# Audio tower on one Trainium2 core: features split 128 + 64 instead of 96 + 96, five matmuls for a product instead of six, router in tiles of 128 tokens

## What is computed

```python
def reference(x, tok_W, tok_b, Wq, Wk, Wv, W_qkv, b_qkv, W_gate, b_gate, A, B_lora, W_proj, b_proj):
    h = einsum('bnf,ef->bne', patches(x), tok_W) + tok_b            # 128 clips, 46 tokens, 192 features
    y = layernorm(h)
    h = h + softmax(causal((y @ Wq) @ (y @ Wk).T)) @ (y @ Wv)
    y = layernorm(h)
    w, idx = top_k(softmax(y @ W_gate.T + b_gate), 2)               # router over 8 experts
    down = einsum('td,nrd->tnr', y, A)                              # 8 experts, rank 16
    qkv = y @ W_qkv.T + b_qkv + 2 * sum_over_chosen(w * (down @ B_lora.T))
    q, k, v = heads(qkv, 12)                                        # 16 features a head
    return h + concat(softmax(q @ k.T / 4) @ v) @ W_proj.T + b_proj
```

## Time and profile before

| | |
|---|---|
| time, median of 3 runs | 698.73 us (697.73 to 700.97) |
| profiled execution | 698.22 us |
| its span, first to last instruction | 696.4 us |
| TensorE busy (share of the span) | 633.9 us (91%) |
| VectorE, ScalarE, GpSimd busy | 521.9, 360.4, 380.7 us |
| mean granted TensorE clock | 0.957 of full speed |

### The profile page before, as it was taken

The page is one execution under the profiler, slowest core; times in us unless marked ns, Lnnn a source line. Parts: engine busy times, 40 slices in busy tenths (PEclk is TensorE's granted clock), DMA queues, the critical chain, the costliest instruction groups (busy, mean ns, idle before and its releaser), DMA issues.

```text
span 696.4 us, 21319 instructions
## 1 busy us (share of the span) xinstructions
PE 633.9 (91%) x8262; PEld 573.4 (82%) x8262; DVE 521.9 (75%) x1365; ACT 360.4 (52%) x670; POOL 380.7 (55%) x634
## 2 busy tenths in 40 slices
PE   2687798999999999999999999999999999977774
PEld 1477788898989898989999898989898988775663
DVE  4352465889788888888888888888878888896662
ACT  2554455666565646565656556565656444533220
POOL 5658876767575666656666666676757322121010
PEclk9999899999999999999999999999999999997755
DMA  9846748675767585848484857666673515251500
GB/s 208 163 92 138 170 92 154 161 125 140 127 156 122 141 140 134 149 114 163 103 176 82 191 88 185 90 173 110 151 123 98 73 43 84 70 80 39 76 26 17
DMA packets 74709, 82.95 MB, mean 119 GB/s; under 512 B 9932, under 2 KB 60016, under 8 KB 74608
## 3 DMA queue, kind: packets, MB, share of 16 engines
q1 hardware_dynamic: 74608, 81.58, 57.7%
HBM read 50.19 MB, written 13.57 MB: 92 GB/s over the span
## 4 chain that ended last, share of the span: by engine, by line
PE 81%; DVE 7%; SPq 4%; POOL 3%; issue 2%; ACT 1%; DMA 1%; DVEq 0%; POOLq 0%; ACTq 0%
PE ps_r L1182 14%; PE ps_r L1184 13%; PE ps_r L1183 13%; PE ps_tok L1182 7%; PE ps_p L1401 6%; PE ps_tok L1183 6%; PE ps_tok L1184 6%; PE ps_s L1389 5%; SPq L393 3%; PE ps_r L1307 3%; PE ps_r L1429 2%; PE ps_r L1318 1%; PE ps_r L1239 1%; DVE p2T L911 1%; DMA xs<-xe 1%
## 5 line engine op out<-in xcount | busy, mean ns | idle before, releaser
L576 POOL TENSOR_TENSOR xs<-raw,xs 90x368 f16<-90x368 f32 x192 | 166.3, 886 | 77.3 <-ACT xs L661 77.3
L1182 PE MATMUL ps_tok<-w_tok,xs 128*128 128x192 f16 x576 | 145.8, 253 | 7.4 <-DMA xs<-xe 4.1
L1184 PE MATMUL ps_tok<-w_tok,xs 128*128 128x192 f16 x576 | 144.5, 251 | 0.0
L1183 PE MATMUL ps_tok<-w_tok,xs 128*128 128x192 f16 x576 | 144.5, 251 | 0.0
L661 ACT ACTIVATE p2T<-ps_p 128x768 f16<-128x768 f32 x64 | 51.9, 810 | 70.0 <-PE ps_r L1184 38.2
L661 ACT ACTIVATE xs<-raw 90x736 f16<-90x736 f32 x96 | 75.3, 805 | 0.0
L1182 PEld LDWEIGHTS ps_tok<-w_tok,xs 128*128 128x128 f16 x576 | 66.4, 115 | 9.8 <-issue 6.8
L1183 PEld LDWEIGHTS ps_tok<-w_tok,xs 128*128 128x128 f16 x576 | 67.1, 117 | 0.2
L1184 PEld LDWEIGHTS ps_tok<-w_tok,xs 128*128 128x128 f16 x576 | 66.4, 115 | 0.2
L911 DVE SCALAR_TENSOR_TENSOR p2T<-ps_p,p2T 128x768 f16<-128x768 f32 x64 | 61.3, 958 | 5.8 <-ACT p2T L661 4.7
L576 POOL TENSOR_TENSOR xe<-raw,xe 90x368 f16<-90x368 f32 x64 | 55.5, 887 | 15.5 <-ACT xe L661 15.3
(11 more groups left out here) (188 smaller groups left out, 2129.1 us busy)
## 6 DMA issues: line engine op xcount, KB each, us to landing
raw<-x SPq DMA_DIRECT2D x32, 1035.0 KB, 7.7
qk_scratch<-qk SPq DMA_DIRECT2D x32, 276.0 KB, 3.1
q<-qk_scratch SPq DMA_DIRECT2D x48, 138.0 KB, 8.4
k<-qk_scratch SPq DMA_DIRECT2D x48, 138.0 KB, 9.0
xs<-xe SPq DMA_DIRECT2D x32, 184.0 KB
v<-v2s SPq DMA_DIRECT2D x64, 73.3 KB
out<-h2b SPq DMA_DIRECT2D x16, 276.0 KB
xs<-xe SPq DMA_DIRECT2D x16, 149.5 KB
```

What stands on the lines that cost most here:

```text
L576: nc.gpsimd.tensor_tensor(lo, src, hi, ALU.subtract).then_inc(s_lo, 1)
L1182: mm(dst, stat[0], mov[0], start=start, stop=False)
L1183: mm(dst, stat[0], mov[1], start=False, stop=False)
L1184: return mm(dst, stat[1], mov[0], start=False, stop=stop)
```

## The change

The features are cut into a chunk of `DA` = 128 and one of `DB` = 64 rows. The chunk of 128 takes three matmuls as before. For the chunk of 64 the high part of the tokens is written twice, into rows 0 to 63 and 64 to 127, and against it stand the high part of the weights (rows 0 to 63) and their low part (rows 64 to 127), so one matmul gives high x high + high x low, and a second one with 64 rows gives low x high (`deep_product`). To have the chunk twice, it is copied behind the 192 features before it is transposed: `xn_twin` and `o2_twin` on ScalarE, `xn2_twin` on GpSimd. `ga_` and `at`, and with them the router's operations, work on three tiles of 128 tokens instead of four pairs. The weights of the second chunk are transposed twice in the units, once to each half of the rows. `LAG`, `RING_AT` and the order of the calls on all engines are new.

```diff
+DA = 128
+DB = D - DA
+CHUNKS = [[(0, 0, DA)], [(0, DA, DB), (DB, DA, DB)]]
...
-STEPS = 23
+STEPS = 24
...
-        w_m = sb("w_m", [DH, 2, 2, D], F16)
+        w_m = sb("w_m", [128, 3, 2 * DA], F16)
...
-        x2T = sb("x2T", [DH, 2, 2, 2, TG], F16)
+        x2T = sb("x2T", [128, 2, 4, TG], F16)
...
-        ga = sb("ga", [PT_, PAIRS, NR + N_EXP])
+        ga = sb("ga", [128, 3, NR + N_EXP])
...
-        UNITS.append(([("m", D * ih, ih) for ih in range(2)], DH, 2 * D, w_m[:, 0, :, :], w_m[:, 1, :, :], WS))
+        for chunk in range(2):
+            blocks = [("m", at, r, (rows_at, n, cols)) for r, rows_at, n in CHUNKS[chunk] for at, cols in ((0, slice(0, D)), (D, slice(DA, D)))]
+            UNITS.append((blocks, 128, 2 * DA, w_m[:, 2 * chunk, :], None if chunk else w_m[:, 1, :], WS))
...
-        N_LOADS = 21
+        N_LOADS = 24
...
+            load(st_v[:, 0:D], Wv[0:DA, :])
+            for r in (0, DB):
+                load(st_v[r:r + DB, D:2 * D], Wv[DA:D, :])
...
-                stack_qk()
-                place_v2()
+                h_to_pairs()
                 store()
-                h_to_pairs()
                 load_next(0)
                 extra_rows()
                 qk_to_scratch()
                 load_next(1)
+                stack_qk()
+                place_v2()
...
+                def xn2_twin():
+                    g = group(s, "xn2_twin")
+                    if g is not None:
+                        pool.wait_ge(s_xn2, g * PAIRS + PAIRS)
+                        nc.gpsimd.tensor_copy(xn2[:, :, D:2 * DA], xn2[:, :, DA:D]).then_inc(s_xn2d, 1)
...
+                def o2_twin():
+                    g = group(s, "o2_twin")
+                    if g is not None:
+                        act.wait_ge(s_o2, g * 8 + 8)
+                        copy(o2[:, :, D:2 * DA], o2[:, :, DA:D]).then_inc(s_o2d, 1)
...
+            def deep_product(dst, stat, mov, start, stop, mov_tokens=False):
+
+                for n, (tokens, weights) in enumerate(((0, 0), (0, 1), (1, 0), (2, 2), (3, 2))):
+                    r = slice(0, DB if tokens == 3 else 128)
+                    a, b = (weights, tokens) if mov_tokens else (tokens, weights)
+                    last = mm(dst, stat(a, r), mov(b, r), start=start and n == 0, stop=stop and n == 4)
+                return last
...
-                def ga_(n):
-                    g = group(s, "ga", n)
+                def ga_():
+                    g = group(s, "ga")
                     if g is not None:
-                        if n == 0:
-                            pe.wait_ge(s_x2T, g * 2 + 2)
-                        bank_free(pe, f"ga{n}", s)
-                        for p in (2 * n, 2 * n + 1):
-                            last = tokens_times(f"ga{n}", p, lambda part, kh: x2T[:, g % 2, part, kh, PT_ * p:PT_ * (p + 1)],
-                                                lambda part, kh: w_ga[:, part, kh, :], NR + N_EXP, (NR + N_EXP) * (p % 2))
+                        pe.wait_ge(s_x2T, g * 2 + 2)
+                        bank_free(pe, "ga", s)
+                        for t, t0 in enumerate(TILES):
+                            last = deep_product(bank("ga")[:, (NR + N_EXP) * t:(NR + N_EXP) * (t + 1)],
+                                                lambda n, r: x2T[r, g % 2, n, t0:t0 + 128], lambda n, r: w_ga[r, n, :], True, True)
                         last.then_inc(p_ga, 1)
```

More of the change, by code:

```diff
@@ L416, in _ @@
             load(b_tok_bc[:], row(tok_b, 128))
-            for kh in range(2):
-                load(b_v[:, kh:kh + 1], b_qkv[2 * D + DH * kh:2 * D + DH * (kh + 1)].rearrange("(p a) -> p a", a=1))
+            for r, n, at, chunk in ((0, DA, 0, 0), (0, DB, DA, 1), (DB, DB, DA, 1)):
+                load(b_v[r:r + n, chunk:chunk + 1], b_qkv[2 * D + at:2 * D + at + n].rearrange("(p a) -> p a", a=1))
             load(b_pr_bc[:], row(b_proj, PT_))
-            load(b_gate_bc[:], row(b_gate, PT_))
+            load(b_gate_bc[:], row(b_gate, 128))
             for t in range(3):
@@ L652, in step @@
                 low(5)
+                low(6)
+                low(7)
+                low(8)
+                ad_()
+                low(9)
+                ln1(0)
+                low(10)
+                low(11)
+                low(12)
+                low(13)
+                low(14)
             for s in range(STEPS):
@@ L690, in _ @@
             act.wait_ge(s_w, 16 * N_LOADS)
-            copy(w_v1[:, 0, :, :], st_v.rearrange("p (a c) -> p a c", a=2), WS).then_inc(s_wd, 1)
+            for chunk in range(2):
+                copy(w_v1[:, 2 * chunk, :], st_v[:, D * chunk:D * (chunk + 1)], WS).then_inc(s_wd, 1)
             def step(s):
@@ L1167, in step @@
                 qk_low(2)
-                max1()
                 max2(2)
                 shift(2)
+                norm2(0)
+                p2t(1)
+                fin(0)
+                h2_(0)
+                max2(3)
+                fin(1)
+                h2_(1)
+                stats2()
+                shift(3)
+                cv_low(0)
+                p2t(2)
+                cv_low(1)
+                h_tile(0)
+                norm2(1)
+                norm2(2)
+                xn_low(0)
+                stats1(0)
+                p2t(3)
+                x2_low(0)
+                x2_low(1)
+                xn_low(1)
+                h_tile(1)
+                norm2(3)
+                stats1(1)
+                logits()
             for s in range(STEPS):
@@ L1282, in sc @@
                         for p in range(PAIRS):
[L1283 to L1287 removed]
+                            last = deep_product(bank("sc")[0:PT_, pair_tokens(p)], lambda n, r: gT[r, n, pair_tokens(p)],
+                                                lambda n, r: xnT[r, g % 2, n, pair_tokens(p)], False, p == PAIRS - 1, mov_tokens=True)
                         last.then_inc(p_sc, 1)
@@ L1338, in at @@
                         bank_free(pe, "at", s)
-                        for p in range(PAIRS):
-                            last = nc.tensor.transpose(bank("at")[0:NR, PT_ * p:PT_ * (p + 1)], ad[:, p, :], ident[0:PT_, 0:PT_])
+                        for t, t0 in enumerate(TILES):
+                            last = nc.tensor.transpose(bank("at")[:, t0:t0 + 128], ad[:, t, :], ident[:])
                         last.then_inc(p_at, 1)
@@ L1485, in step @@
                 xt(0)
+                tok(4)
                 p_(3)
-                ga_(0)
+                yt(0)
+                yt(1)
+                tok(5)
                 xt(1)
-                ga_(1)
-                tok(4)
-                tok(5)
+                tok(6)
+                tok(7)
                 pv(3)
+                ga_()
+                g_(0)
+                v_(0)
+                g_(1)
+                tok(8)
+                tok(9)
+                ot(0)
+                ot(1)
+                tok(10)
+                s_(0)
+                at()
+                sc()
+                tok(11)
+                s_(1)
             for s in range(STEPS):
```

448 lines of the change are left out of this document (202 added, 246 removed), and 14 rows, old and new, of the table LAG.

## The result

The changed kernel takes 757.5 us (median of 4 runs, 756.24 to 767.26), the kernel before beside it on the same chip 699.07 us (697.73 to 700.97). The ratio is 1.087, with a 95% interval of 1.081 to 1.092: it is slower by 8.7%, where 672 us was forecast, 3.8% faster.

What follows compares the result with a forecast made beforehand. TensorE, never waiting in the full steps, was taken as the bound. From 698.2 us: 12 steps x (2.46 - 0.44) = -24.2, ends -3 - 2 - 2.5, before the loop +6, giving 672.5; said 672 us, 8-in-10 range 661 to 685.

Steps and rivals of the forecast that it cites:

- What bounds the kernel: In the full steps, 204.1 to 571.4 us, TensorE never waits, so a matmul less saves its time.
- The matmuls removed: Fewer matmuls per group in `g_`, `qk_`, `v_`, `cv`, `pr`, `sc`, `ga_`: -2.46 us a step, from 36.73 to 34.27 us.
- Depth is free, and I take it to be free for 64 rows too: Matmuls of 192 columns take 82 ns on 96 rows, 83 ns on 128; 64 rows were assumed to cost no more.
- the last sentence of the prediction: Prediction wrong if 64-row matmuls or 128-column loads set a slower pace, VectorE has no idle time, or TensorE waits in more places.
- The wait at `yt(1)`: TensorE waits 0.44 us a step, some 12 times, for the bank `norm2(2)` frees after `h_tile(0)` and `norm2(1)`; bounds 0 and 1.3.
- The costs at nothing: In the steps, ScalarE's and GpSimd's copies are covered by idle time; `ga_`'s loads overlap; its bank's wait about 0 to 0.1 us.
- rival (b): VectorE, at 91% of a step, follows TensorE more closely; waits at further banks, 1 to 2 us a step: 679 to 690; chance 0.17.
- Before the loop: Extra loads, weight transposes and a larger Wq Wk^T product delay the loop's start by +6 us, bounds 3 and 8.
- The term of 12 more transposes: Before the loop, twelve more weight transposes, priced from eight in 1.57 us: +2.4 us.
- The other two terms: Before the loop: three more loads in SP's queue, +1.5 us, and more matmuls in the product Wq Wk^T, +2.9 us.
- The ends: Outside the full steps: first groups up to 132 us -3, step from 571.4 us -2, behind 605 us -2.5 us.
- The sign: Whole kernel: faster by more than 0.5% had chance 0.94, within it 0.02, slower 0.04.

## Why the prediction was wrong, point by point

**What bounds the kernel: right.** A TensorE without waits in the full steps means that its own pace decides. It did so after the change too, and this is why a slower pace of its matmuls told in full.

**The matmuls removed: right.** -2.46 us a step and the wait of 0.44 gave 34.71 us. With all rows in use the full step is 34.83 us, with the wait gone 34.44, against 34.27 in the sum. So five matmuls instead of six are worth 2.29 us a step, 0.17 less than the spacing of the earlier trace rows says; where the 0.17 us go is not shown.

**"Depth is free, and I take it to be free for 64 rows too": the step that failed.** The evidence was 96 against 128 rows, both above 64, and it was carried over to the other side of a border that I hadn't looked for. What the runs showed: depth is free at 72, 96 and 128 rows, and free within a run of matmuls of one kind, but a change between 64 rows or fewer and more than 64 costs 0.20 to 0.25 us for both ways together. 24 of them make 5.46 us a step, more than twice what the change removes. Only the last sentence of the prediction named the case, without a price, and no rival held it; a gap of 0.10 us in and 0.03 us behind the return at `s_(0)` would have given at least 24 x 0.13 = 3.1 us a step, an estimate from those rows alone, and with it a step of 37.8 us, slower than before by 1 us.

The Trainium skill states the rule that I should have weighed: "TensorEngine Tiling (Array Packing)", section "Key Properties", says that changing the tiling mode drains TensorE, and its section "Tiling Modes" lists 128 rows, 64 rows and 32 rows as modes. That an ordinary matmul on 64 rows counts as such a mode is my reading; the border between 64 and 72 rows fits it, and the runs put the price at 0.20 to 0.25 us a visit. No run shows the drain itself. The Trainium skill also says, in "TensorE: Matmul & The Clock Gate", section "LDWEIGHTS (loading the stationary operand)", that a load's time doesn't depend on the rows. That holds for the load by itself, whose row here is 0.11 us with 64 rows and 0.12 with 128; what changes at the seam is when the load starts, no longer ahead of its matmul.

**The wait at `yt(1)`: right**, 4.0 us in 11 waits where 0.44 each was forecast, and it goes with the call that I had named as its cause. Its price is the same with the slow 64-row matmuls (0.36 us) and without them (4.5 us in 12 waits, 0.38).

**The costs at nothing: right.** The copies of the second chunk on ScalarE and GpSimd, the 128-column loads of `ga_` and the third bank's evacuation show up as no wait in the full steps. VectorE never became the bound: with the full step at 34.44 us it is busy for 302.56 of 344.4 us, 88%, where rival (b) had 91%, and TensorE waits for no other engine in these ten steps (view of waits from 201.8 to 546.2 us). Its four waits for VectorE, 2.7 us together, come in the last step, behind 546.2 us.

**Before the loop: mis-sized.** +6 us with bounds of 3 and 8 was forecast, +11.9 measured. The term of 12 more transposes, +2.4 us at 0.2 each, went by transposes only; but the diff sends what lands in rows 64 to 127 through a plain f32 matmul, and a pair takes 0.81 us, so the twelve cost 0.6 each, some 7 us. The other two terms were about right: the weights behind the token weights start 2.0 us later (30.04 for 28.05 us) where 1.5 was forecast, and the product of Wq and Wk takes 2.9 us more. That a plain f32 matmul stands as two rows and takes longer was already in the earlier trace rows, where four of them are "x8" in 2.85 us; it is also why TensorE has 39 rows more before the loop and not some 20. The experiment that takes the twelve away, and with them a third of the matmuls of Wq Wk^T, gave 8.4 us back.

**The ends.** -7.5 us in all was forecast. With all rows, the kernel that the forecast describes, they split as follows. From the first token matmul to the third `mask_b` (52.9 to 134.3 us) it takes 81.4 us where the kernel before takes 90.0, so 8.6 less instead of 3. The twelve steps behind it take 416.4 us for 439.2, 22.8 less instead of 24.2. The last step is 3.3 us shorter instead of 2, the drain 0.9 instead of 2.5.

**The sign.** The forecast of 672 us describes the kernel in which the fifth matmul takes all 128 rows: 675 us. That it comes so near is partly luck: the start of the loop was 4.7 us later than forecast in that run, and the first groups gained 5.6 us more.

## What to carry to other kernels

Among matmuls on more than 64 rows, a single one on 64 or fewer cost more here (0.20 to 0.25 us) than the matmul that it spared (0.04 to 0.16 us): pad it with rows of zeros, or put those on few rows side by side. When a shape is new, look in the trace for the nearest seam between two shapes, not only for a run of equal ones: a gap between the starts of two matmuls counts as busy time and is no wait of TensorE; here it stood, in part, among the waits of its weight loads, as "issue". And a price for "one more of the same" holds only if the new one takes the same instruction; read what the diff issues for each half.

## What the runs showed of the hardware

- A visit of one matmul on 64 or 32 rows among matmuls on 96 or 128 rows costs 0.20 us at 368 columns and 0.25 us at 192. On 72, 96 and 128 rows the full steps are 34.91, 34.96 and 34.83 us, so there it costs next to nothing. As the load isn't ahead of its matmul at these seams, I take the drain to be the mechanism; the runs show the border and the price, not what happens inside.
- TensorE is shown as 99% busy with these gaps in it, because a matmul's row of 250 to 280 ns covers the 0.18 to 0.20 us to the next start. The count of PE falls by 5.5%, and its busy time rises from 633.9 to 690.6 us.
- VectorE reads PSUM and SBUF rows 0 to 63 and writes rows 64 to 127 in one operation at no further price: 0.35 us for the 64x192 low half of `w_pr`, which took 0.36 us with rows 64 to 127 on both sides; this spares TensorE the second copy of a transposed block.
